# A decoder layer on one core: the attention mix spread over three engines, and the second half's norm in the prologue turned early

## The reference

```python
# 1 bilinear and trilinear sums over the tokens, then WO
fwd_r = Q @ V_b * cumsum(K @ W_b);  inv_r = cumsum(invK @ V_b) * (invQ @ W_b)
tri_r = Q @ V_t * cumsum(K @ W_t) * (z @ X_t)          # z: running mean of x
x = x + ((fwd_r + 0.5 * inv_r) @ U_b.T + 0.5 * tri_r @ U_t.T + biases) / counts @ WO.T
# 2 causal attention over the tokens and 77 context rows, with a gate
h = layernorm(x); normed = rmsnorm(h) * norm_w; v = concat([normed, ctx])
attn = softmax(mask((normed @ q_w.T) @ (v @ k_w.T).T / 16)); h_tilde = attn @ v
alpha = sigmoid(h @ gate_w.T + gate_b)
x = x + (1 - alpha) * h + alpha * h_tilde
# 3 feed-forward with blockwise FP4 quantization of activations and weights
x = x + fp4_linear(silu(fp4_linear(n, w_gate)) * fp4_linear(n, w_up), w_down)   # n = layernorm(x)
```

## Time and profile before

| what | value |
|---|---|
| three runs | 588.67, 591.12, 591.13 us; median 591.12 |
| the profiled execution's own time | 588.64 us |
| its span, first to last instruction | 586.9 us |
| PE, DVE, ACT, POOL busy | 92%, 82%, 54%, 50% of the span |
| chain that ended last, by engine | PE 70%, DVE 17%, issue 6%, ACT 4%, POOL 2% |

### The profile page before, as it was taken

One profiled execution on the slowest core, in us unless ns is written; L12 is line 12 of the kernel. 1 busy time (PEld: TensorE's weight loads), 2 busy tenths in 40 slices (PEclk: granted clock), 3 DMA queues, 4 the chain that ended last, 5 costly groups with the idle time before them and its releaser, 6 DMA issues.

```text
span 586.9 us, 10801 instructions
## 1 busy us (share of the span) xinstructions
PE 540.8 (92%) x3156; PEld 473.3 (81%) x3156; DVE 482.6 (82%) x1251; ACT 314.3 (54%) x710; POOL 295.4 (50%) x389
## 2 busy tenths in 40 slices
PE   4969899998999999999988987799999999999995
PEld 4756787887878888878877865699999999999995
DVE  3467789886799867887678968899999999999985
ACT  3234643525544436354444356677777777777652
POOL 4021912618117082361436515877777777777740
PEclk9989899999999999999999999999999999999999
DMA  7620400000000000000000000000000000000001
GB/s 216 194 74 0 150 2 0 2 1 0 0 0 0 0 0 2 0 2 2 0 1 2 0 1 1 2 18 18 18 19 26 18 18 18 18 18 21 25 20 36
DMA packets 16125, 13.78 MB, mean 23 GB/s; under 512 B 3884, under 2 KB 15840, under 8 KB 16096
## 3 DMA queue, kind: packets, MB, share of 16 engines
q1 hardware_dynamic: 16095, 13.43, 7.3%
HBM read 9.23 MB, written 4.19 MB: 23 GB/s over the span
## 4 chain that ended last, share of the span: by engine, by line
PE 70%; DVE 17%; issue 6%; ACT 4%; POOL 2%; DVEq 1%; ACTq 0%; POOLq 0%
PE ps L857 16%; PE ps L858 16%; PE ps L859 16%; PE ps L1052 7%; PE ps L1195 3%; DVE dmix L1365 2%; PE ps L972 2%; PE ps L973 2%; PE ps L1040 2%; DVE X L1369 1%; DVE mx L1350 1%; PE ps L1050 1%; ACT xn_sums L608 1%; DVE parts L1270 1%; PE ps L944 1%
## 5 line engine op out<-in xcount | busy, mean ns | idle before, releaser
L857 PE MATMUL ps<-keys_h,nT_h 128*128 128x256 f32 (+6 forms) x304 | 94.4, 310 | 3.5 <-DVE keys_l L1270 1.8
L858 PE MATMUL ps<-keys_l,nT_h 128*128 128x256 f32 (+6 forms) x304 | 92.1, 303 | 0.0
L859 PE MATMUL ps<-keys_h,nT_l 128*128 128x256 f32 (+6 forms) x304 | 91.8, 302 | 0.0
L857 PE MATMUL ps<-parts,xq_parts 128*128 128x512 f32 (+1 forms) x192 | 77.5, 404 | 7.2 <-DVE xq_parts L1456 7.2
L647 ACT ACTIVATE prob<-ps,nbias 128x205 f32<-128x205 f32 (+7 forms) x32 | 25.7, 805 | 93.2 <-DVE nbias L1352 93.2
L859 PE MATMUL ps<-parts,xq_parts 128*128 128x512 f32 (+1 forms) x192 | 72.0, 375 | 0.0
L858 PE MATMUL ps<-parts,xq_parts 128*128 128x512 f32 (+1 forms) x192 | 71.9, 374 | 0.0
L1052 PE MATMUL ps<-V,probT 128*128 128x256 f32 x288 | 67.4, 379 | 0.0
L857 PEld LDWEIGHTS ps<-keys_h,nT_h 128*128 128x128 f32 x304 | 57.2, 188 | 7.7 <-issue 2.2
L1052 PEld LDWEIGHTS ps<-V,probT 128*128 128x128 f32 x288 | 54.6, 189 | 7.7
L858 PEld LDWEIGHTS ps<-keys_l,nT_h 128*128 128x128 f32 x304 | 57.3, 188 | 3.1
(11 more groups left out here) (205 smaller groups left out, 1506.8 us busy)
## 6 DMA issues: line engine op xcount, KB each, us to landing
X<-in_x_dram SPq DMA_DIRECT2D x8, 512.0 KB, 5.9
out_dram<-X SPq DMA_DIRECT2D x32, 128.0 KB, 1.7
early<-in_L_ffn_w_down_dram SPq DMA_DIRECT2D x1, 704.0 KB, 6.5
early<-in_L_ffn_w_gate_dram SPq DMA_DIRECT2D x1, 640.0 KB, 4.3
early<-in_L_ffn_w_up_dram SPq DMA_DIRECT2D x1, 640.0 KB, 5.1
ctx_rows<-in_ctx_dram SPq DMA_DIRECT2D x1, 308.0 KB
early<-in_L_attn_Winv_dram SPq DMA_DIRECT2D x1, 256.0 KB, 3.9
early<-in_L_attn_WQ_dram SPq DMA_DIRECT2D x1, 256.0 KB, 4.8
```

The costliest lines, as they stand in the source:

```text
L857: mm(o, wh, mh, start=start, stop=False, **kw)
L858: mm(o, wh, ml, start=False, stop=False, **kw)
L859: return mm(o, wl, mh, start=False, stop=stop, **kw)
```

## The change

POOL takes over the part of the mix that has hid in it: it adds hid to X as before (now `sum_half`), and then, per pair of tiles, multiplies hid by the gate and subtracts it from X (`base_tiles`). ACT makes the whole gate, 0.5 tanh + 0.5, by a second operation in place. DVE multiplies pv / sum by the gate and adds it to X. The maximum is written negated as the exp's bias, and SCALE goes into att_wT, so the exp's scale is 1. The third norm's statistics are gathered in a tile of 8 and copied once per batch. In the prologue the second half of batch 0 is normed into a part of hid and turned into banks 0 and 1 before the first half is done, its high and low parts go into the room of the keys; projection tiles 3 and 4 of either half use banks 4 and 5; several weight products and transposes change place and bank. Semaphores mix2 and max go, sum, gated and tanh come; `base` now counts tiles and starts at HALF.

```diff
@@ ACT
             def gate_tile(b, i):
                 act.wait_ge(s_gz, b * TPB + (i + 1))
-                a.activation(th[:, i % HALF, :], gz[:, i % 2, :], ACT.Tanh, scale=0.5).then_inc(s_th, 1)
+                act.wait_ge(s_base, b * TPB + (i + 1))
+                a.activation(th[:, i % HALF, :], gz[:, i % 2, :], ACT.Tanh, scale=0.5).then_inc(s_tanh, 1)
+                act.wait_ge(s_tanh, b * TPB + (i + 1))
+                a.activation(th[:, i % HALF, :], th[:, i % HALF, :], ACT.Identity, bias=half[:, 0:1],
+                             scale=0.5).then_inc(s_th, 1)
...
             def hid_half(b, h):
-                    act.wait_ge(s_mix1, START + (b - 1) * TPB + (h + 1) * HALF)
+                    act.wait_ge(s_base, HALF + (b - 1) * TPB + (h + 1) * HALF)
@@ POOL
+            def base_tiles(b, tiles):
+                pool.wait_ge(s_th, b * TPB + (tiles[-1] + 1))
+                for i in tiles:
+                    g.tensor_tensor(hid[:, i, :], hid[:, i, :], th[:, i % HALF, :], ALU.mult).then_inc(s_gated, 1)
+                pool.wait_ge(s_sum, b * 2 + (tiles[-1] // HALF + 1))
+                wait_apart(4 + tiles[0] // 2, s_gated, b * TPB + (tiles[-1] + 1))
+                for i in tiles:
+                    g.tensor_tensor(X[:, b * TPB + i, :], X[:, b * TPB + i, :], hid[:, i, :],
+                                    ALU.subtract).then_inc(s_base, 1)
...
             def batch(b, more, ahead=False):
-                base_half(b, 0)
+                sum_half(b, 0)
                 values_half(b, 1)
-                base_half(b, 1)
+                base_tiles(b, (0, 1))
+                base_tiles(b, (2, 3))
+                sum_half(b, 1)
                 if not more:
                     rstd3_part(0)
                 raw_scaled(b)
+                base_tiles(b, (4, 5))
                 if more:
                     factors_half(b + 1, 0)
                 raw_rounded(b)
+                base_tiles(b, (6, 7))
@@ DVE, max_tile and mix_tile
-                v.tensor_reduce(mx[:, i:i + 1], flat[:, CTX0:(i + 2) * P], AX.X, ALU.max).then_inc(s_max, 1)
-                ve.wait_ge(s_max, n + 1)
-                v.tensor_scalar(nbias[:, i:i + 1], mx[:, i:i + 1], -SCALE, None, ALU.mult).then_inc(s_neg_max, 1)
+                v.tensor_reduce(nbias[:, i:i + 1], flat[:, CTX0:(i + 2) * P], AX.X, ALU.max, negate=True).then_inc(s_neg_max, 1)
...
-                v.scalar_tensor_tensor(dmix[:, 0, :], ps[:, 5, 0:D], rinv[:, i:i + 1], hid[:, i, :], ALU.mult,
-                                       ALU.subtract).then_inc(s_mix1, 1)
+                ve.wait_ge(s_th, n + 1)
+                v.scalar_tensor_tensor(dmix[:, 0, :], ps[:, 5, 0:D], rinv[:, i:i + 1], th[:, i % HALF, :], ALU.mult,
+                                       ALU.mult).then_inc(s_mix1, 1)
                 ve.wait_ge(s_mix1, START + n + 1)
-                ve.wait_ge(s_th, n + 1)
-                v.scalar_tensor_tensor(dmix[:, 1, :], th[:, i % HALF, :], 1.0, dmix[:, 0, :], ALU.add,
-                                       ALU.mult).then_inc(s_mix2, 1)
-                ve.wait_ge(s_mix2, n + 1)
-                ve.wait_ge(s_base, b * 2 + (i // HALF + 1))
-                v.scalar_tensor_tensor(X[:, n, :], dmix[:, 1, :], 0.5, X[:, n, :], ALU.mult, ALU.add).then_inc(s_x2, 1)
+                ve.wait_ge(s_base, HALF + n + 1)
+                v.tensor_tensor(X[:, n, :], dmix[:, 0, :], X[:, n, :], ALU.add).then_inc(s_x2, 1)
...
-                v.bn_aggr(mv3_tile[:], st3[:]).then_inc(s_aggr3, 1)
-                ve.wait_ge(s_aggr3, n + 1)
-                v.tensor_copy(mv3[:, n, :], mv3_tile[:]).then_inc(s_mean_var3, 1)
+                v.bn_aggr(mv3_batch[:, i, :], st3[:]).then_inc(s_aggr3, 1)
+                if i == TPB - 1:
+                    wait_apart(s_aggr3, n + 1)
+                    v.tensor_copy(mv3[:, bass.ds(b * TPB, TPB), :] if not isinstance(b, int) else mv3[:, b * TPB:(b + 1) * TPB, :],
+                                  mv3_batch[:]).then_inc(s_mean_var3, 1)
@@ PE, prologue
             turn_xn(0, 0, 0)
+            make_proj_w()
             spread_inv_count()
-            make_proj_w()
             pe.wait_ge(w_in[2], 16 * 7)
             turn_weight(2, wo)
-            pe.wait_ge(w_in[3], 16 * 6)
-            turn_weight(3, gw)
             pe.wait_ge(prep_v, 2)
-            proj_tiles(0, (0, 1))
+            proj_tiles(0, (0, 1), (6, 7, 4, 5))
+            turn_xn(0, 1, 1, xn1, 0)
+            pe.wait_ge(s_inv_row, 2)
+            proj_tiles(0, (2, 3), (6, 7, 4, 5))
             make_out_w()
-            proj_tiles(0, (2,))
+            turn_ctx()
             make_att_w()
-            proj_tiles(0, (3,))
             pe.wait_ge(prep_ev, 4)
             y_half(0, 0)
-            turn_ctx()
-            turn_xn(0, 1, 1)
-            proj_tiles(1, range(4))
-            turn_nrm(0, 0)
-            turn_nrm(0, 1)
+            proj_tiles(1, (0, 1), (0, 1, 4, 5), (xnT1_h, xnT1_l))
+            pe.wait_ge(prep_ev, 3)
+            turn_weight(2, gw)
+            proj_tiles(1, (2, 3), (0, 1, 4, 5), (xnT1_h, xnT1_l))
             make_ctx_keys()
+            pe.wait_ge(prep_v, 7)
+            turn_nrm(0, 0, FIRST_NT_BANK)
+            turn_nrm(0, 1, FIRST_NT_BANK)
+            pe.wait_ge(prep_ev, 6)
             y_half(0, 1)
-            pe.wait_ge(prep_v, 6)
             keys_products(0, 0)
@@ DVE, prologue: order behind tri_half(0, 0, 4)
+            low parts of xnT1, both pairs
             att_wT, now times SCALE as well, and att_w
+            x1_half(0, 0)
             att_h and att_l
-            x1_half(0, 0); xnT_low(1)
-            bi_half(0, 1, 1); tri_half(1, 1); nT_low(0, (0, 1)); x1_half(0, 1)
-            low part of gwT
+            low part of gwT
+            bi_half(0, 1, 1, 0); tri_half(1, 1, 4); nT_low(0, (0, 1), FIRST_NT_BANK); x1_half(0, 1)
```

More of the change, by code:

```diff
@@ L88, in decoder_layer @@
         mag_floor = sb("mag_floor", [P, 1])
+        half = sb("half", [P, 1])
         early = sb("early", [P, 9, KD * D])
@@ L181, in decoder_layer @@
         gwT_h, gwT_l = rooms(xq_parts, D, D)
+        xn1 = hid[:, HALF:TPB, :]
+        xnT1_h, xnT1_l = (t[:, :, :].rearrange("p k n -> p (k n)")[:, 0:KD * HTOK].rearrange("p (k n) -> p k n", k=KD)
+                          for t in (keys_h, keys_l))
+        FIRST_NT_BANK = (2, 3)
         prob_flat = prob[:, :, :].rearrange("p a n -> p (a n)")
@@ L409, in _ @@
             after(g.memset(mag_floor[:], GRID_FLOOR))
+            after(g.memset(half[:], 0.5))
             after(g.iota(tok[:], pattern=[[P, TPB]], base=1, channel_multiplier=1))
@@ L754, in _ @@
             a.activation(proj_h[:, :, 5 * R:6 * R], xt[:], ACT.Copy)
-            for h in range(2):
-                act.wait_ge(s_inv_spread, h + 1)
-                a.activation(inv_row[R:2 * R, h * HTOK:(h + 1) * HTOK], ps[R:2 * R, 4 + h, :], ACT.Copy).then_inc(s_inv_row, 1)
+            act.wait_ge(s_rstd1, 2)
+            carry()
+            for i in range(HALF):
+                last = a.activation(xn1[:, i, :], X[:, HALF + i, :], ACT.Identity,
+                                    bias=shift1[:, HALF + i:HALF + i + 1], scale=rstd1[:, HALF + i:HALF + i + 1])
+            last.then_inc(s_xn, 1)
             act.wait_ge(prep_mm, 2)
@@ L952, in proj_tiles @@
                         pe.wait_ge(s_xnT_l, q * 2 + 2)
-                    if t >= 2:
+                    if t >= 2 and banks[0] == banks[2]:
                         pe.wait_ge(s_proj_used, q * 4 + (t - 1))
@@ L980, in turn_nrm @@
                     for t in range(2):
-                        last = turn(ps[:, NT_BANK[j], (k * 2 + t) * P:(k * 2 + t + 1) * P],
+                        last = turn(ps[:, banks[j], (k * 2 + t) * P:(k * 2 + t + 1) * P],
                                     nrm[:, j * 2 + t, k * P:(k + 1) * P], ident[:])
@@ L1277, in xnT_low, with nT_low @@
                         xnT_h[:, :, c]).then_inc(s_xnT_l, 1)
-            def nT_low(b, pairs):
+            def nT_low(b, pairs, banks=NT_BANK):
                 for j in pairs:
@@ L1551, in _ @@
             bi_half(0, 0, 0)
-            tri_half(0, 0)
+            tri_half(0, 0, 4)
+            for j in range(2):
+                c = slice(j * 2 * P, (j + 1) * 2 * P)
+                ve.wait_ge(s_xnT_h, 2 + (j + 1))
+                low(xnT1_l[:, :, c], ps[:, j, :].rearrange("p (k n) -> p k n", k=KD), xnT1_h[:, :, c]).then_inc(s_xnT_l, 1)
             ve.wait_ge(prep_mm, 6)
```

114 lines of the change are left out of this document (60 added, 54 removed).

## The result

The changed kernel takes 574.51 us (median of 4 runs, 571.94 to 574.74). The kernel before took 591.12 beside it (4 runs, 588.67 to 592.18). The ratio is 0.9715, with a 95% interval of 0.9674 to 0.9755: 2.9% faster. The prediction said 574.0, between 566 and 583. The profiled execution took 574.74 us, its span 572.9; before it was 588.64 and 586.9.

What follows compares the result with a forecast made beforehand. PE was taken as the bound, with gains only where others hold it up. Prologue 7.2 plus batches and entry 8.6 made 15.8 us off the profiled 588.64, or 572.9; the forecast was 574, range 566 to 583.

Steps and rivals of the forecast that it cites:

- The prologue: Before the first logits: reordered work starts them at 51.7 instead of 59.15, taken as 7.2 us, bounds 3 and 9.
- PE's wait for gz at 143.09: Middle batch: PE's 1.59 us wait shrinks by 0.6, of which ACT's extra 0.9 takes 0.5 back at 150.30.
- The wait for x1 at 176.26: Middle batch: PE's 1.24 us wait shrinks by 0.9.
- The wait before 339.93: Last batch: PE's 0.64 us wait goes, 0.8 with the slowed start.
- that before 342.67: Last batch: PE's 1.67 us wait shrinks by 0.8 because ACT gets to its copies sooner.
- in (4,5) and (6,7): ACT's Identities in these tile pairs, 0.7 to 1.2 us per pair, are hidden where ACT idles for exps 5 to 7.
- The lock: Rival, chance 0.17: new GpSimd operations block DVE's adds, 12 us in all; batches give nothing, 581.4, or 583 in the median.
- No 2 us STT on th: Sign in the mix on DVE: the operation on th, once blocked to 2.02 us from 0.42, no longer shows that.
- GpSimd late: Rival, chance 0.05: each mix's add waits for GpSimd, 1.5 us per pair, 24 us, giving 597; decides from 1 us per pair.
- 0.7 us slack: First batch: values come some 1 us later than the mix; PE's next projection has this slack.
- Prologue half: Rival, chance 0.12: another clock drop and DVE's longer queue before the second tri leave 3.6 instead of 7.2, 577.
- no effect: Rival, chance 0.04: the prologue's gain is taken back by lock and late GpSimd in part, 587 to 590.

Runs made afterwards that it cites:

- e1: The new prologue with the old mix, against the kernel before: 581.36 us, ratio 0.9862.
- e2: The new mix with the old prologue, against the kernel before: 582.33 us, ratio 0.9831.
- e9: Changed kernel with PE's 16 products that spread 1/count put back ahead of the projection weights' products: 575.88 us, ratio 0.9763.
- e10: e3 with, in the last batch, the fourth weight part's copy on ACT moved ahead of four gate instructions: 570.34 us, ratio 0.9674.
- e3: Changed kernel with ACT's copies of the first two down-weight pieces moved behind its copies of the last probabilities: 572.39 us, ratio 0.9685.
- e4: Changed kernel without ACT's second gate operation (0.5 x + 0.5), so the gate is the bare tanh: 572.39 us, ratio 0.9675.
- e5: Changed kernel with two small DVE steps put back (separate sign turn of the maximum, statistics copied every tile): 579.98 us, ratio 0.9826.
- e11: Changed kernel with the old mix of three DVE operations, the small steps still off DVE: 578.62 us, ratio 0.9791.
- e6: Changed kernel with two more unused GpSimd products per tile, 64 in all: 573.9 us, ratio 0.9722.
- e12: e10 with GpSimd's products and differences of tiles 0 and 1 ahead of the values' second half in every batch: 570.6 us, ratio 0.9636.
- e7: Changed kernel with the projection tiles of each half back on two banks: 575.64 us, ratio 0.9746.
- e8: Changed kernel with the prologue's second half turned late, behind the first output products: 580.44 us, ratio 0.9828.

## Why the prediction was right

**The sum.** 13.9 us were gained between the two profiled executions, 15.8 were predicted (572.9 against 574.74); between the medians it was 16.6, where 574 would have been 17.1. By stage, with a last column from kernels that have no stretch at the lower clock there (e1 against e2, e9 and e10; for the last batch e1 against e2 and e9, since e10 changes it):

| stage | forecast | before to after | at full clock |
|---|---|---|---|
| prologue | 7.2 | 7.6 | |
| first batch | 1.0 | 1.1 | 0.8 |
| second | 1.4 | 2.5 | 2.5 |
| third | 1.2 | 1.8 | 1.9 |
| last | 3.9 | 1.9 | 3.4 |
| entry and FF | 1.1 | -1.0 | 0.6 |

At full clock the batches with the entry gain 9.2 where 8.6 were said: a step of 1.6 that failed and others that gave more than said cancel, which is luck. The profiled execution lost 3.1 of it again to two stretches at the lower clock, 1.6 in the last batch and 1.5 at the end of the feed-forward part.

**The prologue** holds step by step: first projection tile 19.6 said, 19.34 measured; output products 30.2 and 29.89; second half's projection 33.7 and 33.17; 1.2 us idle and 1.12; second output products 43.8 and 43.59; first logits 51.7 and 51.57. The method was to walk the new order with durations of the old trace, and to charge each stretch of PE at full clock where it no longer idles. The clock near 33 stayed up, and the fall near 60 came at 53.7. The first of these numbers is in part luck. With the same order the first tile starts anywhere from 18.14 (e10) to 19.52 (e3), and with the old one at 21.18 (before) and 20.25 (e2). Here is the kernel after, against 3.62 for the same 16 products in e10:

```profile
12.13 4.74 PE L925 MATMUL ps<-prob,early 128*128 128x192 f32 x16
```

In both, the first of these products take 0.53 us each and the rest 0.33; it is 12 that do so in the kernel after and 5 in e10, at a granted clock of 1.00 in the rows of both. What decides it stays open. What holds in every run is the way from the first tile to the first logits: 38.0 us before (up to 1.7 of it the fall near 33), 32.2 to 32.3 in the nine kernels with the whole new prologue, 32.1 in the forecast. The fall of the clock in e9 is no loss that before had: there PE idled 0.88 us before its first tile, with the gate weights' turn in between, and the clock stayed up.

**Middle batches: mis-sized.** What leaves DVE was reckoned right in its lengths (5.7 us less busy in a batch, 5.7 by the rows of the operations); with the gaps the same rows give 8.3, not 8.6. The waits were sized too small. "PE's wait for gz at 143.09 (1.59) shrinks by 0.6, of which ACT's extra 0.9 takes 0.5 back at 150.30": it shrank by 0.95, and only 0.1 came back. e4 shows why the second is so small: without any Identity the batch is 0.07 shorter. ACT's slack before xn was larger than the 0.60 idle that I read; that the exp ahead of it came earlier is my reading, not shown. "The wait for x1 at 176.26 (1.24) shrinks by 0.9": it went, because two savings on VectorE add there to more than their sum (e5, e11).

**The last batch: a failed step.** "The wait before 339.93 (0.64) goes, and that before 342.67 (1.67) shrinks by 0.8 because ACT gets to its copies sooner." Both are unchanged to 0.01 (0.65 and 1.68), so 1.6 us of the forecast did not come. For the second, ACT's two weight copies stand ahead in its own queue and move with the rest; e3 took them away and got 1.0. The first is what the Identities cost (e4), 0.8 us, where I had called them hidden "in (4,5) and (6,7), where it idles for exps 5 to 7": in the last batch a weight copy and `nrm` stand behind the gates, and DVE waits for them ahead of the last maximum. The rest gave more than said: the time up to the second wait 2.8 instead of 2.3, that behind it 0.7 and another 0.6 in the feed-forward part instead of 1.1. Then the clock takes 1.6 back: 60.19 with its stretch from 326.8, at the end of the 1.68 us idle, 58.63 without.

**The feed-forward part** is not touched by an edit, but its entry is: at full clock it takes 235.0 in e1 and 234.5 in e10. The kernel after has 236.0, with three stretches at the lower clock (343.8, 357.5, 558.9) that before had not, each beside an idle stretch of PE (1.94 us before 343.35, and these two):

```profile
356.79 0.50 PE L892 MATMUL ps<-parts,xq_parts 128*128 128x512 f32 x1 [2.27 <-DVE xq_parts L1491]
...
559.03 0.69 PE L1233 MATMUL ps<-ident,probT 128*128 128x128 f32 x2 [2.26 <-DVE probT L1661]
```

They don't weigh the same. Product by product from the part's start, the kernel after is 0.05 us behind e10 until 558 and 1.55 behind from there on: the last stretch costs 1.5, the first two nothing. Waits that e10 has there (1.66 us before 344.87, for one) are gone in the kernel after, so the slower products fill time in which PE would have waited. e3 has only the stretch of the second place and takes 234.5, like e10 with none.

**The rivals.** *The lock* is there, but smaller than before. "No 2 us STT on th" came true by its letter only; the add is locked in its place, DVE and POOL of the kernel after:

```profile
233.68 2.02 DVE L1402 TENSOR_TENSOR X<-dmix,X 128x256 f32<-128x256 f32 x1
```

```profile
233.33 2.10 POOL L498 TENSOR_TENSOR early<-early,wsc 128x1120 f32<-128x1120 f32 x1
```

The Trainium skill (SBUF — State Buffer, "Who interferes with whom") has the later of such a pair block until the earlier one is done, and this row agrees. But the new GpSimd operations are not what locks. An add takes 0.42 undisturbed, and 20 of the 32 do. Six of the twelve longer ones lie beside a raw weights operation of 2.1 us, as above, took 1.09 to 2.02 and lost 7.2 us of 8.7 in all; three beside the new products and differences took 0.64 to 0.83 and lost 0.9; three beside the values lost 0.6. Before, the three operations of this kind per tile (L1365, L1369, L1375) lost 13.0 us. So some 4 us less are lost than before, the rival's 12 us more did not come, and its argument against itself (the blocking is by the long raw operations) was right. An operation of GpSimd took 0.77 where 0.71 to 0.75 were said. *GpSimd late*: true of one tile, the first batch's first. The add waits 1.0 us in the profiled execution, where the lower clock hides it, and 2.4 in e9 and e10, where PE then waits 0.6 to 0.7; the "0.7 us slack" of the prediction did not cover it. e6 shows the point from which I said it decides (1 us per pair) to be wrong, 2.9 don't decide. *Prologue half* and *no effect*: no.

## What to carry to other kernels

Walk a changed prologue instruction by instruction with the old durations; it gave each time within 0.6 us. For a wait at the end of a queue, ask first whether what stands ahead of it on its own engine gets shorter at all: e3 is that question. And judge an edit by stages of equal clock, and hold a run with a stretch at the lower clock against one that has the same stretch: an idle stretch of 1.7 us cost 1.6 again behind it, and a stretch can make a wait vanish that the edit was meant to remove (e12 and e7).

## What the runs showed of the hardware

PE idles some 1.5 us before the first logits in every kernel with the new prologue. The lower clock begins 1.0 to 2.3 us behind the first logits in the kernel after and in e3, e4, e5, e7, e8, e11 and e12, and doesn't come in e1, e6, e9 and e10. e10 and e12 have the same prologue and their first logits at 50.35 and 50.61. What tells them apart stays open. The same holds for the feed-forward part, where e10 has the same idle stretches of 1.93 and 2.27 us and no fall. In the first batch a stretch of 3.41 us costs 0.5 to 0.6 (76.71 to 76.80 in the kernel after, e3 and e8, against 76.17 to 76.20 in e2, e9 and e10), one of 6.83 us 1.4 (77.57 to 77.64 in e4, e7 and e12). The spread between runs of one kernel goes with it. The kernel before ran from 585.56 us at a mean clock of 0.997 to 594.60 at 0.977, e10 from 568.74 at 1.000 to 572.03 at 0.988. One per cent of this kernel's time is thus no property of its code, and a comparison within it wants executions with the same stretches, or stages without any.
